# Reordering the entry, the chunk loop and the exit of a gated linear attention on TensorE, VectorE and ScalarE

## The reference, cut to what matters

```python
xn = layernorm(x)
# layer 0: gated linear attention, 16 heads of 16
q, k, v = xn @ Wq, xn @ Wk, xn @ Wv
gk = log_sigmoid(xn @ Wgk1 @ Wgk2 + bgk2) / 16
for t in range(L):                       # state is 16 x 16 for each head
    state = state * exp(gk[t]) + outer(v[t], k[t])
    out[t] = state @ q[t]
s = (layernorm(out) * gamma + beta) * silu(xn @ Wg) @ Wout
# a mixture of 8 small experts, the best two of each token
gates = softmax(top2(xn @ w_gate))
f = sum_e gates[e] * 0.5 * (relu(xn @ Wd[e] + bd[e]) @ Wu[e] + bu[e])
x = x + s * silu(f)
# layer 1: windowed attention over 64 keys, then a ternary feed-forward net
...
```

## Time and profile before

| | us |
|---|---|
| median of 3 runs | 3802.44 |
| lowest and highest | 3802.12, 3804.59 |
| the profiled execution | 3803.47 |
| its span, first to last instruction | 3801.7 |
| TensorE matmul busy | 3562.5 (94%) |
| VectorE busy | 2682.4 (71%) |
| ScalarE busy | 1898.2 (50%) |
| GpSimd busy | 1084.9 (29%) |

### The profile page before, as it was taken

The page is one execution under the profiler, slowest core; times in us unless marked ns, Lnnn a source line. Parts: engine busy times, 40 slices in busy tenths (PEclk is TensorE's granted clock), DMA queues, the critical chain, the costliest instruction groups (busy, mean ns, idle before and its releaser), DMA issues.

```text
span 3801.7 us, 90111 instructions
## 1 busy us (share of the span) xinstructions
PE 3562.5 (94%) x35196; PEld 2363.2 (62%) x35196; DVE 2682.4 (71%) x6255; ACT 1898.2 (50%) x4311; POOL 1084.9 (29%) x1329
## 2 busy tenths in 40 slices
PE   3999999999999999999989999999999999999999
PEld 2666666666666666666656666666666566666666
DVE  4767677677767767677666776767767777676767
ACT  2264462645536365363643736446264553635536
POOL 3323233232322313223222232323323232231322
PEclk9999999999999999999999999999999999999999
DMA  3000010000100000000000100001000010000000
GB/s 87 1 13 23 2 35 1 14 22 2 34 1 18 18 13 23 2 28 8 13 24 1 31 5 13 23 2 35 1 14 22 2 34 1 17 19 13 23 2 24
DMA packets 72718, 63.37 MB, mean 17 GB/s; under 512 B 18032, under 2 KB 71904, under 8 KB 72288
## 3 DMA queue, kind: packets, MB, share of 16 engines
q1 hardware_dynamic: 72288, 57.52, 5.0%
HBM read 40.72 MB, written 16.78 MB: 15 GB/s over the span
## 4 chain that ended last, share of the span: by engine, by line
PE 19%; issue 14%; POOL 7%; DVE 5%; ACT 5%; POOLq 0%; ACTq 0%; DVEq 0%
PE bank L1587 2%; PE bank L1682 2%; PE bank L1545 2%; PE bank L1699 2%; PE bank L1601 2%; ACT am L933 1%; POOL qx L719 1%; POOL o_rstd L732 1%; POOL o_gam L735 1%; PE bank L1629 1%; DVE am L1141 1%; POOL o_bet L739 1%; POOL end_mask L770 1%; PE bank L386 1%; PE bank L1363 1%
## 5 line engine op out<-in xcount | busy, mean ns | idle before, releaser
L791 POOL TENSOR_TENSOR qx<-qx 128x512 f32<-128x512 f32 x256 | 278.4, 1092 | 677.8 <-ACT qx L1009 676.9
L1329 DVE TENSOR_TENSOR sq_lo<-qx,sq_hi 128x512 fp32r<-128x512 f32 x256 | 208.1, 813 | 198.6 <-ACT sq_hi L988 198.1
L1141 DVE TENSOR_TENSOR am<-bank,causal 128x512 f32<-128x512 f32 x512 | 316.9, 680 | 17.3 <-PE bank L1443 17.3
L1253 DVE TENSOR_REDUCE row_max<-bank 128x4 f32<-128x384 f32 x512 | 270.6, 549 | 79.4 <-PE bank L1587 74.5
L728 POOL TENSOR_SCALAR o_veps<-o_mom 128x1 f32<-128x1 f32 x128 | 28.6, 223 | 881.3 <-DVE o_mom L1211 879.0
L1363 PE MATMUL bank<-w_down,xt 128*128 128x512 f32 x512 | 252.2, 615 | 0.0
L1520 PE MATMUL bank<-w_up,hgt 128*128 128x256 f32 x1024 | 246.2, 381 | 3.6 <-ACT hgt L883 3.6
L1363 PE MATMUL bank<-w_vg,xt 128*128 128x512 f32 x512 | 240.8, 593 | 0.0
L1699 PE MATMUL bank<-sq_hi,pj_t 128*128 128x512 f32 x512 | 214.9, 420 | 16.3 <-DVE sq_lo L1329 9.7
L1260 DVE TENSOR_TENSOR am<-bank,row_max 128x384 f32<-128x384 f32 x384 | 213.9, 557 | 13.2
L830 ACT ACTIVATE decay_in<-bank 128x256 f32<-128x256 f32 x128 | 49.2, 384 | 340.1 <-PE bank L1396 339.9
(11 more groups left out here) (252 smaller groups left out, 8958.0 us busy)
## 6 DMA issues: line engine op xcount, KB each, us to landing
qt<-in_L_attn_x SPq DMA_DIRECT2D x136, 128.0 KB, 2.2
x<-in_L_attn_x SPq DMA_DIRECT2D x128, 128.0 KB, 2.3
out<-x SPq DMA_DIRECT2D x128, 128.0 KB, 1.7
x<-in_L_ffn_w_fc SPq DMA_DIRECT2D x1, 1024.0 KB, 5.5
attn<-in_L_ffn_w_proj SPq DMA_DIRECT2D x1, 1024.0 KB, 7.8
w_up<-in_L_ffn_Wu SPq DMA_DIRECT2D x1, 512.0 KB, 5.9
w_down<-in_L_ffn_Wd SPq DMA_DIRECT2D x2, 256.0 KB, 3.5
w_vg<-in_L_attn_Wv SPq DMA_DIRECT2D x1, 256.0 KB, 4.5
```

What stands on the lines that cost most here:

```text
L791: nc.gpsimd.tensor_tensor(sq[:, n % 3, :], relu[:, n % 3, :], relu[:, n % 3, :], ALU.mult)\
L1141: nc.vector.tensor_tensor(am_tiles[:, :, j], bank[3 + j][:].rearrange("p (f e t) -> p f e t", f=2, e=2), causal[:].unsqueeze(1).unsqueeze( ...
L1253: nc.vector.tensor_reduce(row_max[:, j, :], scored, AX.X, ALU.max, negate=(j == 0))\
L1329: nc.vector.tensor_tensor(sq_lo[:, n % 3, :], sq[:, n % 3, :], sq_hi[:, n % 3, :].bitcast(F32), ALU.subtract)\
```

## The change

- ACT copies projections 2 and 3 before the small exponential of the gates, not behind it.
- DVE makes the decay inputs of the first pair of chunks between the `g_hit` comparisons and the `g_hit` products; the other three pairs stay behind the gates.
- PE projects `w_down` of chunk 0 behind the scores of chunk 0, not ahead of them.
- In every chunk PE makes the state products of both halves first and then the sixteen products of the masked scores. Only the first of them starts the bank anew.
- At the exit PE runs `queries_keys(1)` ahead of the last `output_turn`, `queries_keys(2)` ahead of the last `output_project`, and `chunk_turn(7)` behind the first scores of layer 1. ACT copies the result of `queries_keys(1)` ahead of the last turned output.

```diff
                           .then_inc(s["zexp_ok"], 1)
+                    first_queries_keys(2)
+                    first_queries_keys(3)
                     act.wait_ge(s["top_ok"], at("top_ok", NC + 1))
                     nc.scalar.activation(gexp[:], gdiff[:], ACT.Exp).then_inc(s["gexp_ok"], 1)
-                    first_queries_keys(2)
-                    first_queries_keys(3)
...
                     chunk_turned(6)
+                    queries_keys(1)
                     output_turned(NC - 1)
-                    queries_keys(1)
                     queries_keys(2)
...
+                    decay_inputs(0)
                     dve.wait_ge(s["gsel"], at("gsel", 6))
                     for r in range(2):
                         nc.vector.tensor_tensor(g_hit[:, r], g_hit[:, r],
...
-                    for i in range(NC // 2):
...
+                    for i in range(1, NC // 2):
+                        decay_inputs(i)
...
                     token_major(bank[0][:], 0, w_vg).then_inc(s["vg_ok"], 1)
-                    token_major(bank[2][:], 0, w_down).then_inc(s["hp_ok"], 1)
...
                             parity_scores(0)
+                            token_major(bank[2][:], 0, w_down).then_inc(s["hp_ok"], 1)
...
                         for half in range(2):
                             nc.tensor.matmul(bank[7][:, half * P:(half + 1) * P], state_mid[:, half, :],
-                                             qt[:, half, c * P:(c + 1) * P], start=True, stop=False,
+                                             qt[:, half, c * P:(c + 1) * P], start=(half == 0), stop=False,
                                              skip_group_check=True)
+                        for half in range(2):
                             for e in range(2):
                                 for j in range(4):
...
                     chunk_turn(6)
+                    queries_keys(1)
                     output_turn(NC - 1)
-                    queries_keys(1)
+                    queries_keys(2)
                     output_project(NC - 1)
-                    queries_keys(2)
                     pe.wait_ge(s["f1_ok"], at("f1_ok", NC))
                     low_rank(0)
-                    chunk_turn(NC - 1)
                     pe.wait_ge(s["qk2_ok"], at("qk2_ok", 4))
                     score_masks(0)
                     score_quad(0)
+                    chunk_turn(NC - 1)
                     queries_keys(3)
```

More of the change, by code:

```diff
@@ L1061, in _, with decay_inputs @@
                     dve.wait_ge(s["top_ok"], at("top_ok", 2 * NC + 1))
+                    def decay_inputs(i):
+                        two = slice(2 * i, 2 * i + 2)
+                        dve.wait_ge(s["zln_ok"], at("zln_ok", i + 1))
+                        nc.vector.scalar_tensor_tensor(gk[:, two, :], z[:, two, :], 0.0, zact[:, two, :], ALU.min,
+                                                       ALU.subtract).then_inc(s["gk_ok"], 1)
+                        dve.wait_ge(s["gk_ok"], at("gk_ok", i + 1))
+                        nc.vector.tensor_copy(gk_hi[:, two, :], gk[:, two, :]).then_inc(s["gkh_ok"], 1)
                     nc.vector.tensor_copy(top_f[:], top_i[:, :, 0:2]).then_inc(s["gsel"], 1)
```

## The result

| | before | changed |
|---|---|---|
| median us | 3802.81 | 3732.92 |
| lowest to highest | 3802.12 to 3804.59 | 3732.24 to 3735.63 |
| profiled execution us (its span) | 3803.47 (3801.7) | 3733.54 (3731.8) |

What follows compares the result with a forecast made beforehand. PE's stream was taken to bound the nearly full loop, with holes at entry and exit. Over 16 sequences, loop 40, entry 10 and exit 12 us sum to 62 off 3803.5 (3802.4 by the median): 3741 us, range 3730 to 3752.

Steps and rivals of the forecast that it cites:

- The loop: Chunk loop: grouping both halves' state products saves PE 0.32 us per chunk, 2.5 us per sequence, 40 us in all.
- The crossing: PE in each chunk: switching between tiles and full-array matmuls costs about 0.10 us each way.
- The part of `hg`: Chunks 1 to 6: PE's turns wait for DVE's `hg`, gaining only 0.15 us; `output_turn`'s vanished wait brings 0.31 together.
- Rival B: Loop: crossings not saved, or absorbed by `hg` and `ot`; 3780 us with nothing, 3760 with half; chance 0.15.
- The entry: Entry to chunk 0: first masks start 0.65 us earlier per sequence, 0.25 in each loop turn's first; 10 us in all.
- the sum of the block on DVE: Entry: one gate operation passes before POOL's subtraction, the rest wait for its end; `gk` of pair 1 starts at 556.1.
- The exit: Last chunk into layer 1: `queries_keys(3)` starts 0.73 us earlier, with a new idle of about 0.55; 12 us in all.
- A: Entry: DVE's small gate operations run beside POOL without waiting, so the entry gains 2.0 us; 3719 us, chance 0.13.
- C: Exit gives nothing, as the serial chain to `queries_keys(3)` comes 0.7 us later than summed; 3753 us, chance 0.10.
- E: No effect: all gains end in one unseen wait, for instance for loads; 3800 us, chance 0.04.
- D: Slower: new PE waits lower TensorE's clock for 10 us of work, adding 5 us per sequence; 3821 us, chance 0.04.

Runs made afterwards that it cites:

- the two kernels with the extra product: Changed kernel plus one unused full-array state product per chunk: directly behind the other two, 3760.59 us; between the tiles of the two halves, 3801.99 us.
- The split: Changed kernel with `queries_keys(2)` cut in two, its first half ahead of the last `output_project`, its second behind it: 3737.65 us.
- with `hg` first: Changed kernel with DVE's `y_tok` moved from ahead of `hb` to behind `hg`: 3731.52 us.

## Why the prediction was right, and where its numbers were off

**The loop** was forecast at 2.5 us per sequence and gave 2.6 (1.91 in chunks 1 to 6, 0.34 to 0.35 in chunk 0 and in chunk 7), 41.7 us alone against 40. The crossing was costed from the spacing of records in rows 3, and the two kernels with the extra product show it as a cost of its own. The part of `hg` was right as well: its turns come 0.14 earlier, where 0.15 was forecast, and `output_turn` wins 0.15 more. That the second half came out is partly luck. The prediction moved `ot` and the start of `output_turn` forward by 0.32 together; by its own rows that is 2.64 - 0.32 = 2.32 behind the state products, against 2.33 for the end of the turns of `hg` (1.84 + 0.49). It did not compare the two, and the margin was 0.01; measured it is 0.04. Behind `output_turn` the state update starts 2.56 behind the state products instead of 2.88, so the whole 0.32 arrives there. Rival B, with 0.15 of the chance, pointed at exactly this second waiter.

**The entry** was forecast at 0.65 and gave 1.10. The step that failed is the sum of the block on DVE, a term mis-sized by 0.37: `gk` of pair 1 starts 5.77 behind gdiff, not 6.14. Both `g_hit` products had started before POOL did (the second by 0.03 us, from its end at 546.99 and its length of 0.22), where one was allowed, and POOL's subtraction lasted 1.32 us instead of 1.5: its row holds only the last 0.19 us of that product, and 1.13 behind it. Another 0.07 comes from taking the end of DVE's SiLU row, 561.80, for the time at which the masks could start; with `w_down` alone they start 11.77 behind gdiff, which is 561.73. The mechanism, DVE held until POOL is through, is what the trace shows. A second error lies in what the edits were credited with. The prediction counted from the early decay inputs onward and never asked what the moved `w_down` would do alone, though rows 7 had the answer: DVE was ready 1.11 us before the masks, and moving `w_down` by 1.81 uncovers just that. The runs show 18.4 us for `w_down` alone, 18.6 for all three, and nothing lost without the other two.

**The exit** was forecast at 0.73 and gave 0.80 to 0.81: the idle is 0.46 instead of 0.55. The last `output_project` starts 0.22 later against `queries_keys(0)`, not 0.4, since the sum took the ends of rows where the next start comes earlier. The prediction named two things due at 669.4, PE's own order and the chain over DVE and POOL. The split shows that the first is enough by itself; that the second binds anywhere was not seen.

**Where the 8 us come from.** A sequence that doesn't stand first in a loop turn was forecast to win 2.5 + 0.65 + 0.73 = 3.88 us and wins 4.50. Over 14 of them that is 8.7 us, 6.3 of it from the entry; it is more than 8 since the forecast's 62 was rounded up from 61.3. The two sequences that stand first in a loop turn gave 6.9 us together, as forecast (2 x 3.5). How they share it can't be read: the first `gdiff` of a launch comes at 82.2 to 83.5 us in kernels whose code ahead of that point is the same.

**The rivals.** A (gates beside POOL undisturbed, 3719) falls by line 1090's 1.18 us. B, C and E are out by the three kernels with one part each. D is out by the granted clock of 1.00 in all four stretches, with waits of 0.92 and 0.46 us in them. Its price was also half of what its condition says: by rows 12 matmuls take about twice as long, so 10 us of work add 10 us and not 5.

## What to carry to other kernels

Where a matmul over the whole array and matmuls in column groups alternate, count the alternations: each pair costs a third of a microsecond here, and grouping them is free if the accumulation flags allow it. Before crediting several edits with a gain, read how long the other engine has been ready (the idle time ahead of the waiting instruction): that is what they can win as long as that engine's own queue is not shortened, and the first one that uncovers it leaves nothing for the others. A step moved to fill a hole should be checked for its own turn and copy behind it, since a later place in the same engine's order can cost what an earlier input would win.

## What the runs showed of the hardware

- A crossing from full-array fp32 matmuls to four column groups and back costs 0.32 to 0.34 us per pair (two kernels that differ in nothing but the place of one product: 1.88 and 2.20 us, 41.4 us in the whole time).
- From the end of ACT's copy `yt` out of PSUM to the start of the matmul that waits for it: 0.05 us, in 112 places of each kernel alike. From DVE's masks to the matmul that waits for them: 0.05 to 0.06 us. From ACT's copy `ot` to `output_turn`, where PE waits for it: 0.14 to 0.15 us in every kernel; the cause is open.
- A small group of matmuls that starts from a wait took longer to the next start than the same group in a stream: `output_turn` 0.25 us against 0.21 (with `hg` first and in the changed kernel), `output_project` 0.97 against 0.87 (with `queries_keys(2)` in two halves and in the changed kernel).
- A 128x64 addition of two SBUF inputs on DVE takes 0.23 us while POOL is idle and 1.18 beside POOL's subtraction. The Trainium skill (SBUF — State Buffer, section SBUF: two separate sides) says that whichever of the two starts first keeps the shared ports for its whole instruction. The trace agrees: the second `g_hit` product, just ahead of the addition, had started 0.03 us before POOL's row and kept its usual 0.22 us, and the addition waited for POOL's end.
